# A two-layer Mamba kernel: D moved onto the mask's diagonal, the layer border reordered, halo copies on GpSimd

## The reference, cut to what matters

```python
xc = conv(xBC, conv_w, 4 taps, causal) ; xc = silu(xc + conv_b)      # x, B, C
def step(state, inp):                                                # 4 heads of 128, state 64
    dA = exp(dt_t * A)
    state = state * dA + dt_t * x_t * B_t
    y_t = einsum('bhpn,bn->bhp', state, C_t) + D_param[None, :, None] * x_t
yg = y * silu(z) ; out = (yg * rsqrt(mean(yg * yg) + eps) * norm_w) @ out_proj_w
...
scores = softmax(xt @ Wr) ; G, idx = top_k(scores.T, k)              # experts
```

## Time and profile before

| | |
|---|---|
| median of 3 runs | 1469.93 us |
| the profiled execution's own time | 1473.88 us |
| its span, first to last instruction | 1472.2 us |
| PE, DVE, ACT, POOL busy | 95%, 72%, 53%, 33% of the span |
| granted PE clock, mean | 0.97 of full |
| layer 0 | up to about 721 us of the span |
| layer 1, the loop over 32 tiles | about 721 to 1061 us |
| the experts | from about 1061 us to the end |

### The profile page before, as it was taken

How to read it: one execution, slowest core, us unless ns; L and a number is a source line. 1 busy time by engine, 2 the same in 40 slices (tenths; PEclk the granted TensorE clock), 3 DMA queues, 4 the chain that set the end, 5 groups by cost and what they waited for, 6 DMA issues and landing times.

```text
span 1472.2 us, 23472 instructions
## 1 busy us (share of the span) xinstructions
PE 1397.6 (95%) x7578; PEld 1058.7 (72%) x7578; DVE 1053.1 (72%) x2493; ACT 774.6 (53%) x1612; POOL 487.6 (33%) x599
## 2 busy tenths in 40 slices
PE   7889999999999999999789999999999999999996
PEld 4567768686777768676555655565688898889895
DVE  7889685868769686846589889899865646564642
ACT  4263443526262543526377766887765655465552
POOL 1343334342414234340112221122423544354333
PEclk9799999999999999999799999999999999999998
DMA  7110211203030201211511121121133533343322
GB/s 233 56 58 30 88 43 44 87 0 123 6 108 21 101 28 44 72 35 39 175 40 52 56 69 45 68 73 55 49 82 94 116 74 62 98 108 79 59 46 29
DMA packets 71867, 100.95 MB, mean 69 GB/s; under 512 B 13017, under 2 KB 58209, under 8 KB 71777
## 3 DMA queue, kind: packets, MB, share of 16 engines
q1 hardware_dynamic: 59488, 82.77, 17.3%
q0 software_dynamic: 12288, 17.05, 6.8%
HBM read 74.30 MB, written 25.49 MB: 68 GB/s over the span
## 4 chain that ended last, share of the span: by engine, by line
PE 76%; DVE 12%; ACT 5%; issue 4%; POOL 1%; PEldq 0%; DMA 0%; SPq 0%; DVEq 0%; PEld 0%; ACTq 0%; POOLq 0%
PE bank L2266 70%; DVE am L1753 3%; DVE u L1753 2%; PE bank L2378 1%; DVE E L1773 1%; PE bank L2679 1%; PE bank L2404 1%; DVE hits L2000 1%; PE bank L2621 1%; PE bank L2343 1%; DVE yb L2109 1%; ACT am L1155 1%; ACT tg L1116 1%; PE bank L2560 1%; PE bank L2465 1%
## 5 line engine op out<-in xcount | busy, mean ns | idle before, releaser
L2225 DVE TENSOR_TENSOR aml<-m0big,amh 128x512 fp32r<-128x512 f32 x128 | 88.1, 689 | 175.9 <-ACT amh L1436 175.8
L1033 POOL DMA_INDIRECT out<-EW,IDX x64 | 103.7, 1620 | 219.6 <-DVE EW L2220 205.0
L1431 ACT ACTIVATE m0big<-bank,eb 128x512 f32<-128x512 f32 x128 | 87.9, 687 | 162.4 <-PE bank L2266 146.7
L2266 PE MATMUL bank<-w2h,amh 128*128 128x256 f32 x512 | 147.9, 289 | 0.0
L2266 PE MATMUL bank<-w2h,aml 128*128 128x256 f32 x512 | 144.7, 283 | 0.0
L2266 PE MATMUL bank<-w2l,amh 128*128 128x256 f32 x512 | 144.7, 283 | 0.0
L2266 PE MATMUL bank<-EW,am 128*128 128x256 f32 x512 | 115.8, 379 | 0.0
L1155 ACT ACTIVATE am<-bank,b 128x512 f32<-128x512 f32 x64 | 43.5, 682 | 126.8 <-PE bank L2266 126.1
L2266 PEld LDWEIGHTS bank<-EW,am 128*128 128x128 f32 x512 | 97.2, 190 | 13.5 <-ACT am L1155 0.3
L2266 PEld LDWEIGHTS bank<-w2h,amh 128*128 128x128 f32 x512 | 97.6, 191 | 8.3 <-issue 5.8
L960 POOL TENSOR_TENSOR Xs<-Xsb,lp 128x512 f32<-128x512 f32 x32 | 40.5, 1265 | 188.1 <-ACT Xsb L1207 188.1
(11 more groups left out here) (349 smaller groups left out, 3644.2 us busy)
## 6 DMA issues: line engine op xcount, KB each, us to landing
EW<-in_e_w SPq DMA_DIRECT2D x16, 1024.0 KB, 6.2
dA0b<-dA_d SPq DMA_DIRECT2D x16, 512.0 KB, 3.8
E<-dA_d SPq DMA_DIRECT2D x16, 512.0 KB, 5.3
m0big<-dA_d SPq DMA_DIRECT2D x16, 512.0 KB, 4.8
xin<-in_L_attn_x SPq DMA_DIRECT2D x8, 512.0 KB
xp<-in_L_attn_x SPq DMA_DIRECT2D x8, 512.0 KB, 3.8
rows_d<-xo SPq DMA_DIRECT2D x8, 512.0 KB, 3.1
x_d<-xb SPq DMA_DIRECT2D x8, 512.0 KB, 4.1
```

Source lines behind the costliest of these rows:

```text
L1033: g.indirect_dma_start(out=out_rows, out_offset=bass.IndirectOffsetOnAxis(ap=IDX[:, 4 * u + c:4 * u + c + 1], axis=0), in_=ye[:, q, c, :], ...
L1431: a.activation(am2[:, j % 2, :], bank[j % 2][:, :], ACT.Gelu, bias=eb1[:, u // 2, j:j + 1]).then_inc(gelu_sig.sem, 1)
L2225: v.tensor_tensor(aml[:, j % 4, :], am2[:, j % 2, :], amh[:, j % 4, :], ALU.subtract).then_inc(am_low.sem, 1)
L2266: return t.matmul(out_, lhsT, rhs, start=first, stop=last)
```

## The change

- `XD` is written once, on ACT in the last `step0`, as D times the identity for each of the four heads, from the place where `chunk1(0, 0)` stands. The four copies of each tile on ACT (L1210) go, and so does the DVE addition of `XD` in `sums1` (L2109).
- POOL gets `diagonal1(n+1)` behind `xrows1(n+1)`: it waits for `M` and adds `XD` to the mask, `E` += `XD`, 128x512 with both inputs in SBUF. `intra1` on PE waits for it (`Dd`) where it waited for `M`.
- The five halo copies of a step leave `conv1` on DVE; POOL makes them in one go, `halos1`, in the iterations with c = 2, behind `y_rms1(n-1)`.
- The rounds of the search are 2: 0, 3: 1, 4: 2, 6: 3, ... 20: 14, where they were 1: 0, 2: 1, 3: 2, ... 19: 14. What stood ahead of the loop (a reduction, two copies, the first count) comes behind `sums1(0)`.
- PE makes `z_xt1(0, 1)` inside the last `step0`, ahead of the transposes of `nT`, and no longer behind everything else.

```diff
@@ signals
-        s1.E, s1.M, s1.rv = (sig(n + name, CH) for name in ("decays", "mask_ready", "y_var"))
+        s1.E, s1.M, s1.rv, s1.Dd = (sig(n + name, CH) for name in (
+            "decays", "mask_ready", "y_var", "diagonal_added"))
-        ROUNDS = {1: 0}
-        ROUNDS.update((n, 3 * (n // CH) + n % CH - (n % CH > 0)) for n in range(2, 5 * CH) if n % CH != 1)
+        ROUNDS = dict(zip([n for n in range(2, TILES1) if n % CH != 1], range(15)))
@@ gpsimd
+            def halos1(i):
+                for j in range(5):
+                    blk = (j - 1) % 5
+                    s1.u.wait_ge(pool, i, j + 1)
+                    if i % (STEPS // NB) == STEPS // NB - 1:
+                        ins = g.memset(xbuf[:, blk, 0:3], 0.0)
+                    else:
+                        ins = g.tensor_copy(xbuf[:, blk, 0:3], xbuf[:, blk, T:T + 3])
+                    ins.then_inc(s1.halo.sem, 1)
+
+            def diagonal1(i, c):
+                s1.M.wait_ge(pool, i, c + 1)
+                s1.xd.wait_ge(pool, 0, 1)
+                e = E[:, c % 2, 0:512]
+                g.tensor_tensor(e, e, XD[:, 0, :], ALU.add).then_inc(s1.Dd.sem, 1)
             xrows1(0, 0)
+            diagonal1(0, 0)
+            halos1(0)
             pool.drain().then_inc(phase, 1)
...
                     xrows1(*divmod(n + 1, CH))
+                    diagonal1(*divmod(n + 1, CH))
                 if n + 2 == TILES1:
                     gather(0, 0, 2)
                 if n:
                     y_rms1(*divmod(n - 1, CH))
+                if n % CH == 2 and n + CH < TILES1:
+                    halos1(n // CH + 1)
@@ scalar
-                s1.xsb.wait_ge(act, i, c + 1)
-                for k in range(NH1):
-                    ins = a.activation(XD[:, q, P * k:P * (k + 1)], Xsb[:, q, P * k:P * (k + 1)], ACT.Copy,
-                                       scale=W[1]["D"][:, k:k + 1])
-                ins.then_inc(s1.xd.sem, 1)
...
                     chunk1(0, 0)
+                    for k in range(NH1):
+                        ins = a.activation(XD[:, 0, P * k:P * (k + 1)], ident[:, :], ACT.Copy,
+                                           scale=W[1]["D"][:, k:k + 1])
+                    ins.then_inc(s1.xd.sem, 1)
@@ vector
-                s1.u.wait_ge(dve, i, j + 1)
-                if i % (STEPS // NB) == STEPS // NB - 1:
-                    v.memset(xbuf[:, blk, 0:3], 0.0).then_inc(s1.halo.sem, 1)
-                else:
-                    v.tensor_copy(xbuf[:, blk, 0:3], xbuf[:, blk, T:T + 3]).then_inc(s1.halo.sem, 1)
...
                 s1.t1.wait_ge(dve, i, c + 1)
-                s1.xd.wait_ge(dve, i, c + 1)
-                op(v.tensor_tensor(yb[:, q, :], yb[:, q, :], XD[:, q, :], ALU.add))
                 s1.intra_full.wait_ge(dve, i, c + 1)
...
-            count(0)
+            def first_count():
+                op(v.tensor_reduce(Q8, ident[:, :].rearrange("p (a b) -> p b a", b=NE), AXX, ALU.add))
+                v.tensor_copy(G8.rearrange("p (a b) -> p a b", b=NE),
+                              Q8.unsqueeze(1).to_broadcast([P, P // NE, NE])).then_inc(prepped, 1)
+                s1.sct_full.wait_ge(dve, 0, 1)
+                v.tensor_copy(SCT, YO[:, 0:256]).then_inc(s1.sct.sem, 1)
+                s1.sct.wait_ge(dve, 0, 1)
+                dve.wait_ge(prepped, PREPPED + 9)
+                count(0)
+
             for n in range(TILES1):
...
                 sums1(i, c)
+                if n == 0:
+                    first_count()
@@ tensor
                     in_proj1(0, 0)
+                else:
+                    z_xt1(0, 1)
                 if b is not None:
                     for g in range(2):
                         p = open_back(pe, b, f"nT{g}")
...
             step0(None, STEPS - 1, None)
-            z_xt1(0, 1)
             pe.drain().then_inc(phase, 1)
...
-                s1.M.wait_ge(pe, i, c + 1)
+                s1.Dd.wait_ge(pe, i, c + 1)
```

More of the change, by code:

```diff
@@ L1982, in _ @@
                           ident[0:64, 64:P].unsqueeze(1).to_broadcast([64, 8, 64])).then_inc(bias_steps.sem, 1)
[L1983 to L1989, removed]
             def count(n):
```

## The result

The changed kernel takes 1451.0 us, median of 3 runs (1448.01 to 1452.58), against 1469.93 before: ratio 0.9865, 95% interval 0.9847 to 0.9883. The forecast was 1452.4 us in a range of 1446 to 1463. The profiled execution of the changed kernel took 1451.0 us too, with a span of 1449.3 us. Against the span before that is 22.9 us less, 3.2 of which are not the change's: DVE starts its last `xo` of the first layer, ahead of all changed code, at 706.7 us instead of 709.9.

What follows compares the result with a forecast made beforehand. PE was taken as busy nearly throughout, losing time idling for DVE's S before c = 3 transposes and to the lower clock behind. Terms 4.9 + 2.0 + 11.4 + 0 + 0.2 - 1.0 = 17.5 us gave 1452.4 us, range 1446 to 1463.

Steps and rivals of the forecast that it cites:

- The border, 4.9 and step 0, 2.0: Around the barrier before layer 1's loop: 2.4 and 0.1 us before it, 2.4 behind; step 0 then gains 2.0.
- Barrier and convolution at 718.5 and 729.5: Signs expected in the new profile: last barrier near 718.5, step 0's c = 0 convolution at about 729.5.
- S of c = 2, 1.6 us a step: DVE writes state S in c = 2 earlier: 1.44 from `XD`'s addition, 0.5 from halo copies, less 0.33, so 1.6 us.
- The clock: held in steps 1 and 2, lost in 3 and 6: PE's clock behind the c = 3 idle: 2 x (1.6 + 2.5) + 2 x 1.6 = 11.4 us gained.
- The price of a fall, 2.5 us: From c = 3 transposes to the next tile's: 10.5 us at low clock, 7.7 at full; 2.5 taken per fall.
- Step 4: 0 forecast: The last count, 1.6 us on DVE, enters the iteration whose S PE awaits and eats the 1.6 us gain.
- The end: 1.0 forecast: POOL's addition delays the first expert's token gathers in the last iterations: 1.0 us charged once, bounds 0 and 1.3.
- The stall by the addition, 0.3 us in c = 1: POOL's mask addition holds DVE's `yb` x silu(z) once ahead of S: 0.3 us, bounds 0 and 1.3 each time.
- Halo copies on POOL: nothing: Five copies on POOL after y_rms in c = 2, bounded at 1.6 to 4.5 us, were to cost nothing.
- The slower rival: POOL's addition starts late and blocks DVE 1.3 us in c = 0, 1 and 2: 10.6 us slower, 1480.5 us; chance 0.05.
- Holds every time: Rival: PE's clock never falls, steps 0, 3 and 6 add 2.5, 2.5 and 1.3: gain 23.8, 1446.1 us; chance 0.17.
- My rule of the nearest row: Clock held after 1.06 us idle, fell after 1.97; each predicted c = 3 idle follows the row it is nearer to.

Runs made afterwards that it cites:

- u_z: Changed kernel with `z_xt1(0, 1)` alone put back behind the layer's last transposes: ratio 0.9893 to the kernel before.
- d_alone: Kernel before with D's part of the change alone (`XD` written once, added to the mask on POOL): ratio 0.9948.
- halos_alone: Kernel before with the halo copies moved to POOL alone: ratio 0.9934.
- y_first: Changed kernel with y_rms of tile n-1 ahead of the addition and first gathers in POOL's queue: 1443.5 us, ratio 0.981 to the kernel before.
- u_d: Changed kernel with D's part alone undone (ACT makes `XD` every tile, DVE adds it): ratio 0.9916 to the kernel before.
- y_step0: y_first with an early silu on ACT and rounds leaving out tiles 3, 17, 19 and taking 5, 21: 1440.0 us, ratio 0.979 to the kernel before.
- u_halos: Changed kernel with the five halo copies of the second layer back on DVE: ratio 0.991 to the kernel before.
- u_order: Changed kernel with the old order of `z_xt1(0, 1)`, first count and rounds: ratio 0.9875 to the kernel before.
- y_rounds: y_first with the last three rounds in tiles 17, 18 and 20, none in tile 19: ratio 0.983 to the kernel before.
- y_table: y_first with a 128x1 silu added on ACT at the end of iteration 18: ratio 0.9828 to the kernel before.

## Why the prediction was right, and where it was not

The forecast of 17.5 us met 18.9 by the medians and 19.7 by the steps. The main mechanism held, that S of c = 2 comes earlier and the clock then holds. But several terms were mis-sized, and they cancel: the border with step 0, steps 1 to 3 and step 6 gave 8.0 us more than forecast, step 4 and the end 5.8 us less. That the sum came out so near is luck.

- **The border, 4.9 and step 0, 2.0: 6.9 forecast, 8.8 measured.** The barrier came 3.0 us earlier by the transposes (u_z), against 2.4 and 0.1, but the scan held by POOL took 1.2 of it back. The convolution of step 0 starts 10.66 us behind the barrier (725.59 - 714.93), 13.1 before: 2.4 us as forecast, with that scan in it. Barrier and convolution at 718.5 and 729.5 become, with the early start of 3.2 us taken out, 718.1 and 728.8.
- **S of c = 2, 1.6 us a step.** It came 2.6 us earlier: 31.5 us behind the step's first transposes (791.14 - 759.67), 34.1 before. D's part alone was 1.7 (forecast 1.44 - 0.33), the halo copies 1.3 (forecast 0.5), each by what is lost when it is undone. The copy cost 0.21 us, not 0.1, and the sentence that the stall beside Xs falls on the next DVE instruction failed for c = 1: it fell on POOL. Put on the kernel before alone, D's part brings 1.3 us (d_alone, 32.8 us) and the halo copies 0.9 (halos_alone, 33.2). So each is worth 0.4 us more beside the other; why stays open.
- **The clock: held in steps 1 and 2, lost in 3 and 6.** It held in 3 and 6 too, so steps 1 to 3 gave 14.6 us where 9.8 were forecast, and step 6 gave 2.9 instead of 1.6. The price of a fall, 2.5 us, was right: from the c = 3 transposes to the next ones 10.5 us became 7.9; but a fall that lasts less is worth less, in step 6 8.8 us became 7.7.
- **Step 4: 0 forecast, 2.4 us lost.** The count in front of S was seen. Two things were not. The sum took DVE to enter the step as early as before, but PE's step 3 had become 5 us shorter: DVE's last `x` of step 3 starts 1.7 us behind PE's c = 0 transposes (880.31 against 878.57), where it stood 1.5 us ahead of them (903.69 against 905.19). So S of c = 2 came 35.45 us behind PE's c = 0 transposes, 33.70 before, and the idle grew to 3.02 us. y_first, without the waits for `ry` in step 3, has DVE 0.2 us ahead of PE there and gives 1.7 of the 2.4 back. And I looked at the idle ahead of the transposes only. ACT's table load stood right behind it: of it PE had waited 0.46 us, and waits 1.35 now.
- **The end: 1.0 forecast, 4.4 us lost.** The failed sentence is that `mixed1` is late "while DVE would wait for PE anyway". In the last step DVE doesn't wait for PE: 0.77 us a tile lengthens two tiles from 7.7 to 8.5 us. In iteration 30 two gathers stand ahead of `ry`, as they did before, but they now wait for the addition, which waits for the mask: 3.37 us of waiting. y_first gives 2.5 of the 4.4 back, u_d 3.9. The same sentence failed in steps 1 to 4, where y_first gains 3.3 us more.
- **The stall by the addition, 0.3 us in c = 1.** The group's mean is 0.85 us instead of 0.68, so 0.2 us. By the Trainium skill (SBUF — State Buffer, "SBUF: two separate sides"), whoever of DVE's two-input instruction and GpSimd's starts first keeps the ports for its whole length. The trace agrees: a product that meets only the addition's last part waits 0.2 us for it, the one that starts just behind the addition waits 1.0, and Xs waits for the convolution.
- **Halo copies on POOL: nothing.** Right, and far below the bounds of 1.6 to 4.5 us: 0.67 us for five.

The slower rival did not come about, because what follows the mask on DVE reads PSUM; its mechanism is real. "Holds every time" (23.8 us) was the nearest rival: steps 0 and 4 kept it from being the case.

## What to carry to other kernels

An operation put on an engine off the path is priced by what stands behind it in that engine's queue and by who waits for that; here the swap of two lines in GpSimd's queue was worth 8 us more, nearly half of what the whole change gave. Where a wait hides another, look for the next one behind it before you count the first as gained: in step 4 two cures were worth 0.8 and 0.7 us alone and 3.0 together, in one execution each. And a gain that depends on the granted clock comes per place, not per step: list each idle with what the clock did behind it.

## What was not expected of the hardware

- The length of one idle doesn't tell whether the clock falls. It held behind 1.45 us (step 6), 1.63 (y_step0, step 0), 1.82 (u_halos, step 3) and 1.92 (u_order, step 0), and fell behind 1.41 (y_step0, step 1), 1.43 (u_halos, step 2) and 1.76 (u_halos, step 1). In step 6 the same idle, 2.00 us at the same transposes, is followed by a clock of 1.00 in u_halos (7.66 us to the next transposes) and of 0.53 in d_alone (10.35 us). My rule of the nearest row was no rule. What else decides was not tried. The rows, first u_halos, then d_alone:
```profile
1007.92 0.63 PE L2483 MATMUL bank<-ident,am 128*128 128x128 f32 x4 [2.00 <-DVE S L2136]
1008.00:1011.00 3.00, 2.73 (x19) 1.00 0.13 39
...
1006.15 1.05 PE L2481 MATMUL bank<-ident,am 128*128 128x128 f32 x4 [2.00 <-DVE S L2145]
1006.00:1009.00 3.00, 2.85 (x11) 0.53 0.03 9
```
- The cost of a fall at the same place varies: from step 0's c = 3 transposes to the next ones it is 8.9 us in y_first and 10.7 in y_rounds, whose code is the same up to there. Single executions can't tell 2 us in a step where the clock falls.
- A DVE product of two SBUF inputs, 128x512, took 0.68 us free, 0.87 beside the end of a GpSimd addition and 1.72 when started 0.09 us behind one.
- ACT loads a table when its instruction's own wait has ended, not before: 1.28 us that were idle time until then (920.84, after an idle of 1.46 us). One tiny silu ahead took it off the path in y_table.
